# A transformer block in two parts: GpSimd's work laid out anew over the stages of the attention part

## What is computed

```
x = x + tanh(g_xattn) * cross_attention(layernorm(x), ctx, ctx)     # 8 batches of 512 x 256, 16 heads of 16
x = x + tanh(g_ffn) * block(layernorm(x))
block(x):  h = x + attention(rmsnorm(x, g1), wq, wk, wv, wo)       # rotary positions, causal
           y = h + moe(rmsnorm(h, g2), w_router, wg, wu, wd)       # 8 experts of 704, top 2
```

## Time and profile before

| | us |
|---|---|
| median of 3 runs | 1704.07 (1696.66 to 1710.51) |
| the profiled execution | 1700.58 |
| its span, first to last instruction | 1698.8 |
| first block / second block, parted at | about 1158 |
| TensorE busy | 1484.0 (87%) |
| VectorE busy | 986.9 (58%) |
| GpSimd busy | 968.2 (57%) |
| mean granted clock of TensorE | 0.936 |

### The profile page before, as it was taken

How to read it: one execution, slowest core, us unless ns; L and a number is a source line. 1 busy time by engine, 2 the same in 40 slices (tenths; PEclk the granted TensorE clock), 3 DMA queues, 4 the chain that set the end, 5 groups by cost and what they waited for, 6 DMA issues and landing times. The chain is left out here.

```text
span 1698.8 us, 33170 instructions
## 1 busy us (share of the span) xinstructions
PE 1484.0 (87%) x9936; PEld 942.4 (55%) x9936; DVE 986.9 (58%) x2347; ACT 782.5 (46%) x1781; POOL 968.2 (57%) x1288
## 2 busy tenths in 40 slices
PE   2999998898998998998998996743999999999997
PEld 1232334344344444444334454422999999999997
DVE  4887757658768768767756654231444444444443
ACT  1475654564664664664554563411333333333332
POOL 7465856955966966966858665541334334433343
PEclk9798999899999999999998998756999999999999
DMA  7555366554654664554653545216142443244211
GB/s 200 148 149 167 94 180 179 168 156 137 175 178 139 170 187 140 175 181 132 173 175 102 163 132 166 103 62 248 54 148 60 155 148 122 94 151 154 59 57 31
DMA packets 112509, 238.42 MB, mean 140 GB/s; under 512 B 20623, under 2 KB 74771, under 8 KB 110294
## 3 DMA queue, kind: packets, MB, share of 16 engines
q1 hardware_dynamic: 76050, 147.65, 29.3%
q0 software_dynamic: 22656, 78.48, 13.6%
q10 hardware_dynamic: 13636, 10.18, 2.2%
HBM read 144.14 MB, written 93.14 MB: 140 GB/s over the span
## 5 line engine op out<-in xcount | busy, mean ns | idle before, releaser
L953 DVE TENSOR_REDUCE neg<-max_ps 128x1 f32<-128x512 f32 (+3 forms) x1024 | 565.1, 586 | 325.2 <-PE max_ps L638 191.2
L843 ACT ACTIVATE probs<-key_ps 128x512 f32<-128x512 f32 (+3 forms) x1024 | 500.0, 519 | 407.6 <-PE key_ps L655 207.8
L635 PE MATMUL max_ps<-k_stack,q_stack 96*128 96x512 bf16 (+3 forms) x1024 | 367.1, 362 | 41.0 <-DVE neg L953 26.7
L652 PE MATMUL key_ps<-q_stack,k_stack 99*128 99x512 bf16 (+3 forms) x1024 | 359.0, 352 | 21.1 <-ACT probs L843 15.6
L635 PEld LDWEIGHTS max_ps<-k_stack,q_stack 96*128 96x128 bf16 x1024 | 102.7, 100 | 260.5 <-DVE neg L953 171.1
L1633 PE MATMUL y_ps<-weights,hidden_t 128*128 x1278 | 172.5, 291 | 4.8 <-issue 3.4
L652 PEld LDWEIGHTS key_ps<-q_stack,k_stack 99*128 99x128 bf16 x1024 | 103.0, 101 | 126.5 <-ACT probs L843 64.3
L1633 PEld LDWEIGHTS y_ps<-weights,hidden_t 128*128 128x128 f32 x1278 | 159.7, 196 | 6.7 <-issue 6.7
L1609 PE MATMUL gate_ps<-weights,rows_t 128*128 x852 | 156.1, 332 | 6.7 <-DMA weights<-w_split 4.2
L1533 DVE TENSOR_TENSOR hidden<-silu,up_ps 128x352 f32<-128x352 f32 x142 | 74.1, 522 | 137.2 <-PE up_ps L1609 137.1
L1480 POOL TENSOR_TENSOR more<-part,so_far 128x256 f32<-128x256 f32 x71 | 51.9, 731 | 175.6 <-issue 122.4
(11 more groups left out here) (203 smaller groups left out, 2190.1 us busy)
## 6 DMA issues: line engine op xcount, KB each, us to landing
w_split<-w_parts POOLq DMA_DIRECT2D x32, 704.0 KB
weights<-w_split SPq DMA_DIRECT2D x8, 2816.0 KB, 10.9
weights<-w_split SPq DMA_DIRECT2D x8, 1280.0 KB, 13.1
...
```

Of the source, the lines that this page charges most:

```text
L635: r = mm(ps[:, 0:keys], q_stack[g][0:KROWS, hd, qt * P:(qt + 1) * P], k_stack[g][0:KROWS, hd, 0:keys], start=True, stop=not own)
L652: r = mm(ps[:, q0:S], k_stack[g][0:KROWS + NEGROWS, hd, kt * P:(kt + 1) * P], q_stack[g][0:KROWS + NEGROWS, hd, q0:S], start=True, stop=no ...
L843: act.activation(probs[:, kt % 2, hd, q0:S], key_ps[j % 2][:, q0:S], ACT.Exp).then_inc(m["exp_done"], 1)
L953: v.tensor_reduce(neg[:, g % 2, hd, qt:qt + 1], max_ps[(n * 16 + j) % MAX_RING][:, 0:keys], op=ALU.max, axis=AX.X, negate=True).then_inc(m ...
```

## The change

The tables move work of GpSimd between stages, and in `body` the order within a stage is new. Scatters and `values` stand behind `split_neg`; `x_rows` behind the splits of x and context; rotations in front of `x1_rows` in every stage. `pos_i` and `weight` get a second set, so that VectorE's wait is for the scatters of one batch earlier. The seven padding stores are spread over steps 1 to 5. The turns of the context in steps 1 to 4 stand at units 26 and 30 instead of 18 and 22. The tables' entries for single batches near the end, which are cut here, move by a few units in the same way: batch 4's output work in step 5 some 10 to 13 units later, batch 6's query projection 20 earlier.

```diff
-C_TURNS = {1: at(-1, 10, 14), 2: at(-1, 66, 70), 3: at(0, 52, 56), **{b: at(b - 3, 18, 22) for b in range(4, B)}}
-X1_SUMS = {b: at(b - 2, 112, 128) for b in BATCHES} | {0: at(-1, 112, 114), 1: at(0, 46, 48), LAST: at(LAST - 2, 112, 114)}
+C_TURNS = {1: at(-1, 26, 30), 2: at(-1, 66, 70), 3: at(0, 52, 56), **{b: at(b - 3, 26, 30) for b in range(4, B)}}
+X1_SUMS = {b: at(b - 2, 124, 128) for b in BATCHES} | {0: at(-1, 112, 114), 1: at(0, 46, 48), LAST: at(LAST - 2, 112, 114)}
...
-HN2_TURNS = {b: at(b + 1, 93, 97) for b in BATCHES} | {LAST - 2: at(LAST - 1, 90, 94), LAST - 1: at(LAST, 18, 22), LAST: at(LAST, 78, 82)}
-LOGITS = {b: at(b + 1, 101) for b in BATCHES} | {LAST - 2: at(LAST - 1, 98), LAST - 1: at(LAST, 27), LAST: at(LAST, 87)}
+HN2_TURNS = {b: at(b + 1, 90, 94) for b in BATCHES} | {LAST - 3: at(LAST - 2, 94, 98), LAST - 1: at(LAST, 18, 22), LAST: at(LAST, 78, 82)}
+LOGITS = {b: at(b + 1, 98) for b in BATCHES} | {LAST - 3: at(LAST - 2, 102), LAST - 1: at(LAST, 27), LAST: at(LAST, 87)}
...
-XQ_STAGE = {b: stage(b - 4, 5) if b > 2 else stage(-1, 2) for b in range(2, B)}
+XQ_STAGE = {b: stage(b - 4, 4) if b > 2 else stage(-1, 2) for b in range(2, B)}
...
-C_STAGE = {1: stage(-1, 1), 2: stage(-1, 5), **{b: stage(b - 3, 3 + (b == 3)) for b in range(3, B)}}
-V_STAGE = {1: stage(-1, 1), **{b: stage(b - 3, 7) for b in range(2, B)}}
+C_STAGE = {1: stage(-1, 2), 2: stage(-1, 5), **{b: stage(b - 3, 3 + (b == 3)) for b in range(3, B)}}
+V_STAGE = {1: stage(-1, 1), **{b: stage(b - 3, 5) for b in range(2, B)}}
...
-    {b: (stage(i, s), stage(i, s), stage(i, s + 1), stage(i, s + 1)) for b, i, s in ((0, 0, 1), (LAST - 1, LAST - 2, 5), (LAST, LAST - 1, 1))}
+    {b: (stage(i, s), stage(i, s), stage(i, s + 1), stage(i, s + 1)) for b, i, s in ((0, 0, 1), (LAST, LAST - 1, 1))} | \
+    {LAST - 1: (stage(LAST - 2, 4), stage(LAST - 2, 4), stage(LAST - 2, 5), stage(LAST - 2, 6))}
-BASE_STAGE = {b: stage(b + 1, 7) for b in BATCHES} | {LAST - 2: stage(LAST - 1, 5), LAST - 1: stage(LAST, 1), LAST: stage(LAST, 5)}
-SCATTER_STAGES = {b: (stage(b + 2, 4), stage(b + 2, 6)) for b in BATCHES} | \
-    {LAST - 4: (stage(LAST - 2, 4),) * 2, LAST - 3: (stage(LAST - 1, 3),) * 2, LAST - 2: (stage(LAST - 1, 7),) * 2,
-     LAST - 1: (stage(LAST, 3), stage(LAST, 4)), LAST: (stage(LAST, 7),) * 2}
-PIECES_IN_STEP = {-1: (0, 0, 1, 1, 1, 0, 1, 1), 0: (2, 0, 0, 0, 1, 2, 2, 2), LAST - 2: (0, 0, 2, 3, 1, 0, 0, 1),
-                  LAST - 1: (1, 0, 0, 1, 2, 2, 3, 2), LAST: (0,) * 8}
+BASE_STAGE = {b: stage(b + 1, 5) for b in BATCHES} | {LAST - 1: stage(LAST, 1), LAST: stage(LAST, 5)}
+SCATTER_STAGES = {b: (stage(b + 2, 5), stage(b + 2, 6)) for b in BATCHES} | \
+    {LAST - 4: (stage(LAST - 2, 2), stage(LAST - 2, 3)), LAST - 3: (stage(LAST - 1, 2), stage(LAST - 1, 3)),
+     LAST - 2: (stage(LAST - 1, 7), stage(LAST, 0)), LAST - 1: (stage(LAST, 4),) * 2, LAST: (stage(LAST, 7),) * 2}
+PIECES_IN_STEP = {-1: (0, 0, 1, 1, 1, 1, 1, 1), 0: (2, 0, 0, 0, 1, 2, 2, 1), LAST - 2: (0, 0, 1, 2, 1, 0, 1, 1),
+                  LAST - 1: (1, 0, 1, 2, 3, 2, 2, 1), LAST: (0,) * 8}
...
-    count = lambda n: PIECES_IN_STEP.get(n // 8, (0, 0, 0, 2, 2, 1, 1, 2))[n % 8]
+    count = lambda n: PIECES_IN_STEP.get(n // 8, (0, 0, 0, 2, 3, 2, 1, 0))[n % 8]
...
-                    if i == 0:
-                        for n in range(SPARE):
+                    if 0 < i < LAST - 1:
+                        for n in range((i - 1) * SPARE // (LAST - 2), i * SPARE // (LAST - 2)):
...
-                        over(dve, m["scat"], b * (2 * QT * 16))
-                        chain.link(v.tensor_copy(pos_i[:, :], pos_f[:, :]))
+                        over(dve, m["scat"], (b - 1) * (2 * QT * 16))
+                        chain.link(v.tensor_copy(pos_i[:, b % 2, :], pos_f[:, :]))
```

More of the change, by code:

```diff
@@ L1372, in body @@
                             split("k", "c", flat_k, b)
+                        for b, _ in due(XQ_STAGE, now):
+                            x_rows(b)
                         for b, _ in due(BASE_STAGE, now):
                             base_rows(b)
-                        for b, _ in due(V_STAGE, now):
-                            values(b)
                         ng = Step(step.i + 1).neg_of(0) if s == 7 else step.neg_of(s + 1)
@@ L1381, in body @@
                             split_neg(step, ng)
+                        for b, _ in due(V_STAGE, now):
+                            values(b)
+                        for b, k in due(SCATTER_STAGES, now):
+                            scatter(b, k)
                         for n in pieces_in(now)[-1:]:
```

40 lines of the change are left out of this document (16 added, 24 removed).

## The result

The changed kernel takes 1716.38 us (median of 9 runs, 1712.33 to 1719.04), the kernel before 1701.06 in the same comparison (9 runs, 1693.25 to 1710.51). The ratio is 1.0088, with a 95% interval of 1.0070 to 1.0107: slower by a little under 1%. The profiled execution of the changed kernel took 1715.59, its span 1713.8 against 1698.8. So the forecast of 1721 missed by 5, and its sum, +16.8, stands against +15.0 of the spans. That agreement is in good part luck: it hides errors of both signs, and the rest of this text is about them.

The account below looks back on a forecast made before the run. TensorE's waits for late GpSimd, 44 us, were taken as what to win. Terms -9.4 - 9 + 37.9 - 6.4 + 1 + 2.7 = +16.8 on 1700.6 gave 1717.4, plus 3.5 for the median: 1721, range 1692 to 1742.

Parts of the forecast that it names:

- The trip, and the third piece: Stage x.4, steps 1 to 4: three weight pieces, about 8.2 us apart, delay `hn2_rows` and TensorE at unit 90; +37.9.
- The clock's price: Extra TensorE time at lower clock after one long wait: 1.9 us, from stage 1.1 against 2.1, charged in four steps.
- The -9.4: Stage 1.1: the last piece of step 0 ends earlier, so 24.4 us falls to about 15.0; -9.4.
- the -9: Steps 2 to 5: small waits go because no piece stands in front of the rotation; -9 us.
- Step 5: Batch 3's scatters leave stage 5.4, pieces 2, 3, 1 become 1, 2, 1; two waits for the maxima's split go; -6.4 us.
- Step 6: Three pieces in stage 6.4 bring waits of 10.9 and 8.5 us; three old waits, 18.2, go; +1.
- The tail: Last step: both batch 6 scatters in stage 7.4, so one scatter and a landing precede `base_rows`; +2.7 us.
- Rival (b): Stages x.7: VectorE may catch up while TensorE waits, giving back at most 3 us a step; 1709 us; chance 0.18.

Follow-up runs that it names:

- experiment 5's last kernel: Changed kernel with two `w_in` and `w_parts` buffers, batch 6's scatters in 7.3 and 7.4, pieces moved x.4 to x.7 and 6.4 to 6.7: 1662.51 us, ratio 0.9735.
- Experiment 2: Kernel before with only the changed kernel's piece counts in steps 1 to 4 (three in x.4); run once, no total given, x.4 with x.5 +30.1 us.
- experiment 4: Changed kernel with the old piece counts of steps 1 to 4 (two in x.4, two in x.7): 1713.88 us, ratio 1.0027 to the kernel before.

## Why the prediction was right, and where it was not, point by point

*The trip, and the third piece.* Right, and shown: rows and instants as computed, and the trip taken away takes 38.8 with it. The term was too small all the same (37.9 against 46.8). Most of that is the waits themselves: for the split and `hn` together TensorE stood 9.6, 9.2, 11.1 and 5.9, 35.9 instead of 30.3, since trips were 8.05 to 9.2 and not 8.2 throughout, and step 3 was later still. The clock's price, read from one stage as 1.9, was 2.7, 2.6, 1.6 and 2.7 in busy time against the same stages without a wait (experiment 5's last kernel), 9.6 instead of 7.6. The moved turn of `hn2`, 0.3 a step, had no term. That makes the 46.8. That the wait for the split is part of the delay and not added to it was right: in 2.5 unit 90 came 9.2 late, 8.01 of it for `hn`.

*The -9.4 and the -9* came as -8.3 and -8.3. Experiment 2 gives -10.6 for the second from the counts alone, so the reason named, no piece in front of the rotation, was the right one. What the forecast didn't see is that this gain and the loss in x.4 are tied (experiment 4).

*Step 5*, -6.4 forecast and 0.2 measured. The term itself came: the waits for the split shrank to 0.8 and 1.0, and 5.4 with 5.5 lost 5.9. But 5.2 with 5.3 became 4.0 longer, 1.9 of it busy time of TensorE, and 5.7 lasts 20.9 instead of 16.8, with 3.6 of waits for VectorE's maxima instead of 1.8 and a clock of 0.84 instead of 1.00. The step that failed is that the tables' entries for single batches were costed at nothing: batch 4's output work, 9 to 10 units later (not 10 to 13), and batch 6's query projection, which left 5.4 for 5.3. Which of them does it was not tried.

*Step 6* came as +3.9 instead of +1: 13.9 and 7.1 in 6.5 where 10.9 and 8.5 stood, and a stage of 37.0 at a clock of 0.63.

*The tail*: the mechanism was right, the size not (2.7 against 6.1). The sum ended at the first scatter (3.0 there in fact); the second one's landing took 1.2 to 1.3 longer, and more behind it.

*What had no term at all*: -8.9 in step -1 and -18.5 in x.6 and x.7. A part of the first could be read: one row of the kernel before, 7.31 for `ctx_in`, at the very unit that the diff moves; the text named the context's turns as an edit that moves no work. Taken alone that edit brings 1.1, so the order of `x_rows` and the split of the context had to be read along with it. Of the second, x.7 has 10.8, and that too could be read: 4.9 us in each x.7 of VectorE instructions that last six to nine times their usual length. The text had costed moved work by GpSimd's time and by who waits for GpSimd, and not by what runs beside it. The 8 of x.6 is one execution's, as said above. Rival (b), that part is given back in x.7 by at most 3 a step, has the place and the size (some 2.7 a step in x.7), but for a reason that didn't happen: the gain is there whether or not TensorE waits, as experiment 5's last kernel shows.

So 1721 was near 1716 by luck: a gain of 27 was overlooked, and losses of 9, 7, 3, 3 and 3 with it.
